# Decoder layer in fp32: softmax shift and sum moved into eight exponentials a unit

## The chip, the cores and the metric

One core of one Trainium2 chip runs the whole program. The metric is the device time in microseconds (us); lower is better. The engines are called PE (TensorE, matrix products), DVE (VectorE), ACT (ScalarE), POOL (GpSimd) and SP (SyncE, which issues the DMAs). They run their own instruction streams and meet through semaphores.

## The reference, cut to what matters

A post-norm decoder layer on x of shape (4, 256, 512): a masked dense product with gelu, a cross attention with 32 query and 8 key heads over 64 context positions, and a linear layer with routed low-rank additions, each followed by a residual sum and a normalization. All in fp32. The attention is the part that the change touches:

```
q = apply_rope((query @ wq) by head); k = apply_rope(key @ wk), v = value @ wv, each repeated 4 times
scores = einsum('bhqd,bhkd->bhqk', q, k) / sqrt(128)
attn   = softmax(scores + mask[:, None, :, :], axis=-1)      # over 64 keys
out    = einsum('bhqk,bhkd->bhqd', attn, v) ... @ wo
x = layernorm(x + out)
```

The softmax subtracts the row's maximum, takes the exponential and divides by the row's sum.

## The kernel before, in words

The program is one function, `decoder_layer`, with a block of instructions for each engine. The order on every engine is written out by hand, and each step waits for semaphores that count finished steps. Every fp32 product is three products of a high and a low part (`mm3`, lines 259 to 263), so most operands are split: ACT copies the high part (the `_hi` steps), DVE or POOL subtracts it to get the low part (the `_lo` steps).

The attention runs over eight head groups g = 0 to 7 (LAST is 7), one key head and four query heads each. Group 0 is written out ahead of the loop, groups 1 to 6 are turns of a loop (`Fori(1, LAST)`), and group LAST is written out behind it. A turn works on group g and finishes group g - 1. A group has four units u = 0 to 3 (two heads by one half of the 1024 tokens). For each unit:

- `query(g, u, f)`, f = 0 and 1: 12 matmuls of 512 columns on PE. `q_copy` (ACT), `q_sin` (POOL), `q_cos` and `q_rot` (DVE) apply the rotary embedding. f = 1 always uses PSUM bank 2, so the next one waits for `q_rot` of the last.
- `scores` (one unit) or `score_pair` (two): 64 matmuls of 64x64 a unit into banks 4 and 5.
- `mask_scores` (L1275, DVE, in place in PSUM), `row_max` (L1280), `shift` (L1287, subtracts the maximum, PSUM to the SBUF tile SM), `exps` (L897, ACT, one exponential of 512 columns), `row_sum` (L1292), `row_inverse` (L1296), then `probs` (L1728, POOL, multiplies by the inverse). The 512 columns of a unit are eight rows of 64 keys: four token tiles by two heads.
- `probs_transpose` (PE, four transposes), `pt_hi` (ACT) and `pt_lo` (DVE).

`value_out(g, n, b)`, n = 0 to 7, is 3 matmuls into bank b, which `vw_hi` (two ACT copies) and `vw_lo` (two DVE subtractions) split. `attend(g, t)`, t = 0 to 7, is 6 matmuls into a bank of A_BANKS, which `accumulate(g, t)` (DVE, L1314) adds to X. `keys` and `values` are 12 matmuls of 256 columns; `k_swap`, `k_sin`, `k_cos`, `k_add` and `k_spread` (four ACT copies) and `v_hi`, `v_lo` work on what they leave.

Behind the last group stand: `stats` and `guess` (DVE), `newton` and `mean_shift` (POOL) and `normalize` (ACT) for the second normalization; `weight_transpose` with `f_hi`, `f_lo`; `x2_tile(t)` (PE, four transposes) with `x2_hi` and `x2_lo`; `base(t)` (12 matmuls), `lora_in`, `lora_out(t)` (3 matmuls); then `out_add`, `stats(2, t)`, `guess(2, m)` on DVE, `newton(2, m)` on POOL for m = 0 to 2 and on DVE for m = 3 (in `out_last`), and the stores. `newton(2, 3)` waits for `newton(2, 2)`.

Of the kernel before, what the change touches and what calls it, by code (L numbers as in the profile page):

```python
# [12 lines left out]
ALU = mybir.AluOpType  # L13
# [18 lines left out]
def decoder_layer(nc, x, ctx_in, amask, w1, w2, b2, smask, wq, wk, wv, wo, fW, fb, fA, fB, rW, rb, rope, out):  # L32
# [24 lines left out]
    with ExitStack() as es:  # L57
# [51 lines left out]
        T_BANKS, A_BANKS = (7, 6, 7, 6), (6, 3, 6, 6, 6, 6, 3, 6)  # L109
# [5 lines left out]
        q_mm q_cp q_cos q_sin q_rot s_mm s_masked s_max s_sub s_exp s_sum s_inv p_done  # L115
# [43 lines left out]
        def x2_bank(t):  # L159
            return (5, 4, 3, 4, 3, 5, 3, 5)[t]  # L160
# [11 lines left out]
        def y_bank(t):  # L172
            return 2 + t % 2

# [83 lines left out]
        def _(pe):  # L258
# [214 lines left out]
            w2_transpose(3)  # L473
# [46 lines left out]
            pe.wait_ge(sm["tr_lo"], 8)  # L520
            values(0)
# [5 lines left out]
            dense(7)  # L527
            pe.wait_ge(sm["k_cos"], 1)
            query(0, 0, 0)
            pe.wait_ge(sm["tr_lo"], 14)  # L530
            value_out(0, 0, 7)
            pe.wait_ge(sm["x_added"], 7)
            query(0, 0, 1)
            pe.wait_ge(sm["tr_lo"], 13)
            x1_tile(4, 14)
            pe.wait_ge(sm["x_added"], 8)
            value_out(0, 1, 3)
            pe.wait_ge(sm["vw_lo"], n_vw(0, 0))
# [8 lines left out]
            pe.wait_ge(sm["tr_lo"], 15)  # L547
            x1_tile(6, 16)
            pe.wait_ge(sm["tr_lo"], 16)
            x1_tile(7, 17)  # L550
            pe.wait_ge(sm["q_rot"], n_rot(0, 0, 1))
            query(0, 1, 1)
            pe.wait_ge(sm["k_cos"], 1 + 1)
            query(0, 2, 0)
            pe.wait_ge(sm["tr_lo"], 18)
            value_out(0, 2, 7)
            pe.wait_ge(sm["vw_lo"], n_vw(0, 1))
            value_out(0, 3, 3)
            pe.wait_ge(sm["q_rot"], n_rot(0, 1, 1))
            query(0, 2, 1)  # L560
            pe.wait_ge(sm["vw_lo"], n_vw(0, 2))
# [3 lines left out]
            pe.wait_ge(sm["vw_lo"], n_vw(0, 3))  # L565
# [3 lines left out]
            pe.wait_ge(sm["s_sub"], n_unit(0, 0))  # L569
            scores(0, 1)  # L570
            pe.wait_ge(sm["pt_lo"], n_unit(0, 0))
            value_out(0, 5, 7)

            with pe.Fori(1, LAST) as g:
                pe.wait_ge(sm["k_cos"], g + 1)
                query(g, 0, 0)
                pe.wait_ge(sm["s_sub"], n_unit(g - 1, 1))
                score_pair(g - 1, 3)
                pe.wait_ge(sm["q_rot"], n_rot(g - 1, 3, 0))
                values(g)  # L580
                pe.wait_ge(sm["x_added"], n_added(g - 2, 7))
                probs_transpose(g - 1, 1)
                pe.wait_ge(sm["vw_lo"], n_vw(g - 1, 4))
                value_out(g - 1, 6, 3)
                pe.wait_ge(sm["q_rot"], n_rot(g - 1, 3, 1))
                query(g, 0, 1)
                pe.wait_ge(sm["pt_lo"], n_unit(g - 1, 1))
                attend(g - 1, 0)
                pe.wait_ge(sm["vw_lo"], n_vw(g - 1, 5))
                value_out(g - 1, 7, 7)  # L590
# [1312 lines left out]
```

## Time and profile before

| what | value |
|---|---|
| median of 3 runs | 492.2 us (491.89 to 492.32) |
| profiled execution, its own time | 492.99 us |
| its span (first to last instruction) | 491.2 us |
| mean granted clock of TensorE | 0.985 |
| busy: PE, DVE, ACT, POOL | 473.9, 408.3, 260.6, 273.4 us |
| read from HBM, written | 29.15 MB, 2.10 MB |

The profile is one execution. A row of a group names a line of the kernel, the engine, the operation and its tiles with their shapes, then how often it ran, its busy time, the mean time of one and the idle time of the engine just before it with what ended that. In a timeline each row has its start in the span, its duration, and in brackets the idle time before it and the step that ended it. The duration of a matmul is modelled and longer than the distance from one start to the next. The granted clock is a share of 2.4 GHz.

### The profile page before, as it was taken

The page shows a single profiled execution, that of the slowest core. Times are in us where ns is not written, and L with a number is a line of the kernel's source. Part 1 is how long each engine was busy: PE and PEld are TensorE (multiplying, and loading weights), DVE is VectorE, ACT ScalarE, POOL GpSimd, SP SyncE. Part 2 cuts the span into 40 slices and gives each one's busy share as a digit, 9 for nine tenths or more (in the row PEclk, how much of TensorE's full clock was granted, in tenths as well). Part 3 has the DMA queues.
Part 4 walks back from the last instruction along what each step waited for, and adds up shares of the span by engine and source line. Part 5 has one row for each costly group of instructions (what it writes and reads, how often), then busy time and mean ns, then how long its engine had stood idle before and what let it go on. Part 6 is the DMA issues. An engine that isn't in the chain of part 4 may idle for free.

```text
span 491.2 us, 11126 instructions
## 1 busy us (share of the span) xinstructions
PE 473.9 (96%) x4189; PEld 395.9 (81%) x4189; DVE 408.3 (83%) x739; ACT 260.6 (53%) x462; POOL 273.4 (56%) x347
## 2 busy tenths in 40 slices
PE   8999999999999999999999999999999999879991
PEld 8888778888888888888888888888888788668781
DVE  2779898988987898798979987988799889988585
ACT  4574447735673566365735663575458254353423
POOL 3477637854674467456636672676366423156523
PEclk9999999999999999999999999999999999979996
DMA  8943300240023011402040212022002400000013
GB/s 274 353 146 93 124 1 1 87 130 1 2 85 128 0 22 63 128 0 80 7 127 0 85 34 94 0 85 85 0 0 87 67 1 2 1 0 2 0 40 133
DMA packets 29137, 31.56 MB, mean 64 GB/s; under 512 B 6321, under 2 KB 16817, under 8 KB 29114
## 3 DMA queue, kind: packets, MB, share of 16 engines
q1 hardware_dynamic: 29114, 31.25, 20.1%
q8 instruction: 15, 0.25, 0.2%
q14 instruction: 8, 0.07, 0.0%
HBM read 29.15 MB, written 2.10 MB: 64 GB/s over the span
## 4 chain that ended last, share of the span: by engine, by line
PE 77%; DVE 9%; SPq 4%; POOL 3%; issue 3%; DMA 2%; ACT 1%; ACTq 0%; POOLq 0%; DVEq 0%
PE bank L261 23%; PE bank L263 22%; PE bank L262 22%; PE bank L369 6%; PE bank L393 3%; SPq L205 2%; DMA WQr<-in_L_xattn_wq_dram 2%; DVE X L1223 1%; DVE BST L1187 1%; PE bank L267 1%; POOL NW L1711 1%; DVE VWl L1139 1%; POOL NW L1709 1%; POOL RS L1713 1%; POOL NW L1707 1%
## 5 line engine op out<-in xcount | busy, mean ns | idle before, releaser
L1722 POOL TENSOR_TENSOR QS<-QS,SIN 128x512 f32<-128x512 f32 x64 | 83.0, 1297 | 124.4 <-ACT QS L801 124.4
L261 PE MATMUL bank<-XTh,WQh 128*128 128x512 f32 x256 | 101.7, 397 | 0.7 <-DVE XTl L1139 0.7
L263 PE MATMUL bank<-XTh,WQl 128*128 128x512 f32 x256 | 100.0, 391 | 0.0
L262 PE MATMUL bank<-XTl,WQh 128*128 128x512 f32 x256 | 99.7, 390 | 0.0
L1139 DVE TENSOR_TENSOR VWl<-bank,VWh 64x512 fp32r<-64x512 f32 x128 | 88.0, 688 | 9.3 <-ACT VWh L801 7.4
L801 ACT ACTIVATE QS<-bank 128x512 f32<-128x512 f32 x64 | 38.3, 598 | 103.1 <-PE bank L263 102.6
L801 ACT ACTIVATE VWh<-bank 64x512 fp32r<-64x512 f32 x128 | 75.9, 593 | 23.5 <-PE bank L263 20.9
L1251 DVE TENSOR_TENSOR bank<-bank,COS 128x512 f32<-128x512 f32 x64 | 44.6, 697 | 23.2 <-ACT QS L801 22.6
L261 PEld LDWEIGHTS bank<-XTh,WQh 128*128 128x128 f32 x256 | 48.1, 188 | 11.5 <-issue 1.3
L263 PEld LDWEIGHTS bank<-XTh,WQl 128*128 128x128 f32 x256 | 48.0, 188 | 10.5
L262 PEld LDWEIGHTS bank<-XTl,WQh 128*128 128x128 f32 x256 | 48.1, 188 | 9.5
L261 PE MATMUL bank<-VWh,PTh 128*128 128x512 f32 x128 | 50.9, 398 | 0.4 <-DVE X L1314 0.3
L262 PE MATMUL bank<-VWl,PTh 128*128 128x512 f32 x128 | 50.3, 393 | 0.0
L263 PE MATMUL bank<-VWh,PTl 128*128 128x512 f32 x128 | 50.1, 392 | 0.0
L1314 DVE TENSOR_TENSOR X<-X,bank 128x512 f32<-128x512 f32 x64 | 43.2, 674 | 7.2 <-PE bank L263 6.3
L1698 POOL TENSOR_TENSOR WOl<-WOr,WOh 128x512 fp32r<-128x512 f32 x32 | 41.3, 1291 | 12.1 <-ACT WOh L801 11.6
L1263 DVE TENSOR_TENSOR QR<-bank,QS 128x512 f32<-128x512 f32 x64 | 42.9, 683 | 0.4
L1688 POOL TENSOR_TENSOR WQl<-WQr,WQh 128x512 fp32r<-128x512 f32 x32 | 41.0, 1304 | 2.1 <-ACT WQh L801 2.1
L369 PEld LDWEIGHTS bank<-KK,QR 64*64 64x64 f32 x2048 | 31.6, 135 | 5.9 <-issue 5.8
L1728 POOL TENSOR_TENSOR SM<-SM,RI 128x512 f32<-128x512 f32 x32 | 33.5, 1046 | 3.8 <-DVE RI L1296 3.8
L369 PE MATMUL bank<-KK,QR 64*64 64x64 f32 x2048 | 34.2, 220 | 0.0
L261 PEld LDWEIGHTS bank<-VWh,PTh 128*128 128x128 f32 x128 | 24.3, 190 | 6.0 <-DVE X L1314 1.0
(150 smaller groups left out, 965.1 us busy)
## 6 DMA issues: line engine op xcount, KB each, us to landing
WQr<-in_L_xattn_wq_dram SPq DMA_DIRECT2D x8, 1024.0 KB, 5.5
WOr<-in_L_xattn_wo_dram SPq DMA_DIRECT2D x8, 1024.0 KB, 5.4
KVr<-in_L_xattn_wk_dram SPq DMA_DIRECT2D x8, 256.0 KB, 5.4
KVr<-in_L_xattn_wv_dram SPq DMA_DIRECT2D x8, 256.0 KB, 5.5
out_dram<-X SPq DMA_DIRECT2D x8, 256.0 KB, 2.0
X<-in_x_dram SPq DMA_DIRECT2D x3, 512.0 KB, 9.9
WQr<-in_L_attn_w_dram SPq DMA_DIRECT2D x4, 256.0 KB, 4.9
WOr<-in_L_attn_w_dram SPq DMA_DIRECT2D x4, 256.0 KB, 5.1
```

Source lines behind the costliest of these rows:

```text
L261: pe.matmul(o, lh, rh, start=start, stop=False)
L262: pe.matmul(o, lh, rl, start=False, stop=False)
L263: return pe.matmul(o, ll, rh, start=False, stop=stop)
L369: m = pe.matmul(s_tiles(u)[part, a, t, :], QR[head, u % 2, f, t * P + part.start:t * P + part.stop], KK[head, b, f, :], start=f == 0, stop ...
L801: return act.activation(o, i, ACT.Copy)
L1139: return dve.tensor_tensor(o, i, f32(hi), ALU.subtract)
L1251: dve.tensor_tensor(q, q, by_pos(COS, 2, S), ALU.mult).then_inc(sm["q_cos"], 1)
L1263: dve.tensor_tensor(QR[:, u % 2, f, :], bank[:, q_bank(u, f), :], QS[:, u % 2, 1 - f, :], ALU.add if f else ALU.subtract).then_inc(sm["q_r ...
L1314: dve.tensor_tensor(X[:, t, :], X[:, t, :], bank[:, A_BANKS[t], :], ALU.add)\
L1688: pool.tensor_tensor(wq_split(WQl, h), wq_head(WQr, h), f32(wq_split(WQh, h)), ALU.subtract)\
L1698: pool.tensor_tensor(WOl[:, h, :], WOr[:, h, :], f32(WOh[:, h, :]), ALU.subtract)\
L1722: pool.tensor_tensor(q, q, SIN[:, :].unsqueeze(1).broadcast_to([P, 2, S]), ALU.mult)\
```

## The change

The unit's softmax on DVE and ACT is arranged anew. `mask_scores` writes the masked scores to SBUF (the tile CTX, free after the context has been transposed) instead of back to PSUM. `row_max` reads them there and gives the negated maximum. `shift` and `row_sum` are gone. `exps` is eight exponentials of 64 columns, each with its row's negated maximum as bias and its sum as a second output; `row_inverse` waits for them. PE waits for `s_masked` where it waited for `s_sub`. Beside this the hand-written order of all engines is a new one, and PSUM banks are dealt out anew: all transposes of probabilities go to bank 7, and attends, value products and the transposes at the end use other banks. The matmuls are the same in number and shape.

The functions, then places of the new order that the prediction speaks of:

```diff
-        T_BANKS, A_BANKS = (7, 6, 7, 6), (6, 3, 6, 6, 6, 6, 3, 6)
+        T_BANKS, A_BANKS = (7, 7, 7, 7), (6, 6, 3, 7, 7, 7, 6, 3)
...
+        def masked_rows(u):
+
+            return CTX[:, u % 2, :].rearrange("p (a t k) -> p a t k", a=2, k=KS)
...
             def exps(g, u):
-                act.wait_ge(sm["s_sub"], UNITS * g + u + 1)
-                act.activation(SM[:, u % 2, :], SM[:, u % 2, :], ACT.Exp).then_inc(sm["s_exp"], 1)
+
+                act.wait_ge(sm["s_max"], n_unit(g, u))
+                if counted(UNITS * g + u - 1):
+                    act.wait_ge(sm["t_mm"], UNITS * g + u - 1)
+                for r in range(8):
+                    t, a = r // 2, r % 2
+                    m = act.activation(SM[:, u % 2, r * KS:(r + 1) * KS], masked_rows(u)[:, a, t, :], ACT.Exp,
+                                       bias=MX[:, u % 2, 4 * a + t:4 * a + t + 1], accum_out=SU[:, u % 2, r:r + 1])
+                m.then_inc(sm["s_exp"], 1)
...
-                s = s_tiles(u)
+                if counted(UNITS * g + u - 1):
+                    dve.wait_ge(sm["s_exp"], UNITS * g + u - 1)
...
-                dve.scalar_tensor_tensor(out=s, in0=s, scalar=1.0 / math.sqrt(DK), in1=m, op0=ALU.mult, op1=ALU.add)\
+                dve.scalar_tensor_tensor(out=masked_rows(u), in0=s_tiles(u), scalar=1.0 / math.sqrt(DK), in1=m, op0=ALU.mult, op1=ALU.add)\
...
-                dve.tensor_reduce(MX[:, u % 2, :].rearrange("p (a t) -> p a t", a=2), s_tiles(u), AX_X, ALU.max).then_inc(sm["s_max"], 1)
-
-            def shift(g, u):
...
+                dve.tensor_reduce(MX[:, u % 2, :].rearrange("p (a t) -> p a t", a=2), masked_rows(u), AX_X, ALU.max, negate=True).then_inc(sm["s_max"], 1)
+
+            def row_inverse(g, u):
                 dve.wait_ge(sm["s_exp"], UNITS * g + u + 1)
-                dve.tensor_reduce(SU[:, u % 2, :], sm_rows(u), AX_X, ALU.add).then_inc(sm["s_sum"], 1)
```

The turn of the loop in the changed kernel, by engine, without the waits (g1 is g - 1):

```
PE:  query(g,0,0) attend(g1,1) score_pair(g1,3) value_out(g1,7) query(g,0,1) values(g) attend(g1,2) attend(g1,3)
     query(g,1,0) probs_transpose(g1,2) value_out(g,0) query(g,1,1) probs_transpose(g1,3) query(g,2,0) value_out(g,1)
     attend(g1,4) score_pair(g,1) value_out(g,2) attend(g1,5) query(g,2,1) attend(g1,6) attend(g1,7)
     probs_transpose(g,0) value_out(g,3) query(g,3,0) value_out(g,4) query(g,3,1) probs_transpose(g,1) keys(g+1)
     value_out(g,5) value_out(g,6) attend(g,0)
ACT: q_copy(g,0,0) k_spread(g) vw_hi(g1,7) exps(g1,2) v_hi(g) q_copy(g,0,1) exps(g1,3) wo_hi(g,3) wkv_hi(g+1)
     q_copy(g,1,0) pt_hi(g1,2) vw_hi(g,0) q_copy(g,1,1) pt_hi(g1,3) q_copy(g,2,0) vw_hi(g,1) vw_hi(g,2) exps(g,0) ...
DVE: q_cos(g,0,0) accumulate(g1,1) mask_scores(g1,2) row_max(g1,2) mask_scores(g1,3) row_max(g1,3) vw_lo(g1,7)
     row_inverse(g1,2) v_lo(g) q_cos(g,0,1) accumulate(g1,2) accumulate(g1,3) q_rot(g,0,0) row_inverse(g1,3) q_rot(g,0,1) ...
```

The hand-over behind the last scores, before and after:

```
PE before:  scores(L,3) attend(L,3) value_out(L,5) value_out(L,6) weight_transpose(2) value_out(L,7) weight_transpose(3)
            probs_transpose(L,3) x2_tile(0) x2_tile(1) weight_transpose(4) attend(L,4) base(0) attend(L,5) ...
PE after:   scores(L,3) weight_transpose(1) probs_transpose(L,2) attend(L,0) weight_transpose(2) value_out(L,4) attend(L,1)
            weight_transpose(3) attend(L,2) value_out(L,5) weight_transpose(4) attend(L,3) value_out(L,6)
            probs_transpose(L,3) value_out(L,7) x2_tile(0) attend(L,4) attend(L,5) attend(L,6) attend(L,7) x2_tile(1) base(0) ...
DVE after:  mask_scores(L,3) row_max(L,3) f_lo(1) pt_lo(L,2) accumulate(L,0) stats(1,0) row_inverse(L,3) f_lo(2)
            accumulate(L,1) vw_lo(L,4) stats(1,1) accumulate(L,2) guess(1,0) f_lo(3) vw_lo(L,5) accumulate(L,3) stats(1,2)
            vw_lo(L,6) pt_lo(L,3) stats(1,3) vw_lo(L,7) guess(1,1) x2_lo(0) accumulate(L,4) ...
ACT after:  ... pt_hi(L,2) exps(L,3) f_hi(2) vw_hi(L,4) f_hi(3) vw_hi(L,5) f_hi(4) vw_hi(L,6) pt_hi(L,3) vw_hi(L,7) normalize(1,0) ...
```

At the end, and in the head:

```diff
             lora_out(2)
             lora_out(3)
+            pe.wait_ge(sm["fy_out"], 2)
+            base(6)
             lora_out(4)
             lora_out(5)
-            pe.wait_ge(sm["fy_out"], 2)
-            base(6)
-            lora_out(6)
             pe.wait_ge(sm["fy_out"], 4)
             base(7)
+            lora_out(6)
             lora_out(7)
...
             out_add(3)
+            stats(2, 3)
+            guess(2, 1)
             out_add(4)
-            stats(2, 3)
+            stats(2, 4)
             out_add(5)
-            stats(2, 4)
-            guess(2, 1)
             stats(2, 5)
+            guess(2, 2)
             out_add(6)
-            guess(2, 2)
...
             dense(6)
-            pe.wait_ge(sm["tr_lo"], 8)
-            values(0)
+            pe.wait_ge(sm["tr_lo"], 7)
+            keys(0)
```

## Rows read from the trace of the kernel before

**Rows 1.** Page: busy time by engine; slices of PE and of its clock.
```profile
PE 473.9 (96%) x4189; PEld 395.9 (81%) x4189; DVE 408.3 (83%) x739; ACT 260.6 (53%) x462; POOL 273.4 (56%) x347
...
PE   8999999999999999999999999999999999879991
...
PEclk9999999999999999999999999999999999979996
```

**Rows 2.** Busy time of PE, PEld, DVE, ACT, POOL in two stretches, then granted clock.
```profile
183.77:231.05 47.28, 47.28 (x468) 39.70 (x471) 40.49 (x67) 26.61 (x49) 28.44 (x24) 1.00 0.18 55
433.00:439.00 6.00, 5.37 (x21) 5.01 (x22) 4.75 (x10) 3.55 (x6) 3.00 (x3) 0.50 0.00 0
```

**Rows 3.** Timeline of PE around the last scores and after: start, duration.
```profile
423.32 1.16 PE L369 MATMUL bank<-KK,QR 64*64 64x64 f32 x64
...
429.93 0.50 PE L261 MATMUL bank<-WOh,VTh 128*128 128x512 f32 x1 [1.69 <-DVE VWl L1139]
...
433.63 1.08 PE L393 MATMUL bank<-ID,SM 128*128 128x128 f32 x4 [2.30 <-POOL SM L1728]
...
442.19 0.39 PE L261 MATMUL bank<-VWh,PTh 128*128 128x512 f32 x1
442.42 0.39 PE L262 MATMUL bank<-VWl,PTh 128*128 128x512 f32 x1
```

**Rows 4.** Chain that ended last: start, time in it, of 64 small matmuls and 4 transposes.
```profile
84.52 1.09 PE bank L369 x64
...
92.88 0.44 PE bank L393 x4
```

**Rows 5.** Timeline of DVE in the same stretch: start, duration, idle before.
```profile
424.63 0.69 DVE L1275 SCALAR_TENSOR_TENSOR bank<-bank,MSK 128x512 f32<-128x512 f32 x1
425.23 0.68 DVE L1187 BATCH_NORM_STATS2 BST<-X 128x6 f32<-128x512 f32 x1
...
426.05 0.66 DVE L1280 TENSOR_REDUCE MX<-bank 128x8 f32<-128x512 f32 x1
...
427.82 0.16 DVE L1196 TENSOR_SCALAR VE<-MV 128x2 f32<-128x2 f32 x1
...
428.48 1.39 DVE L1139 TENSOR_TENSOR VWl<-bank,VWh 64x512 fp32r<-64x512 f32 x2
429.91 0.69 DVE L1292 TENSOR_REDUCE SU<-SM 128x8 f32<-128x512 f32 x1
...
439.65 0.69 DVE L1314 TENSOR_TENSOR X<-X,bank 128x512 f32<-128x512 f32 x1 [1.75 <-PE bank L263]
```

**Rows 6.** Groups of DVE by line: busy us, mean ns of one, idle before.
```profile
L1275 DVE SCALAR_TENSOR_TENSOR bank<-bank,MSK 128x512 f32<-128x512 f32 x32 | 22.2, 692 | 2.0 <-PE bank L369 1.8
L1287 DVE TENSOR_TENSOR SM<-bank,MX 128x512 f32<-128x512 f32 x32 | 21.9, 684 | 0.3
...
L1292 DVE TENSOR_REDUCE SU<-SM 128x8 f32<-128x512 f32 x32 | 21.6, 676 | 0.8 <-ACT SM L897 0.7
```

**Rows 7.** Groups of ACT: exponential, short copies, one with two pointers, shortest one.
```profile
L897 ACT ACTIVATE SM<-SM 128x512 f32<-128x512 f32 x32 | 20.0, 626 | 5.3 <-DVE SM L1287 5.3
...
L801 ACT ACTIVATE KK<-KC 64x256 f32<-64x256 f32 x32 | 13.3, 416 | 9.0 <-PE bank L369 7.7 <-POOL KC L1742 1.0
...
L926 ACT ACTIVATE X<-X,NM,RS 128x512 f32<-128x512 f32 x8 | 6.2, 808 | 10.2 <-POOL NM L1760 10.2
...
L931 ACT ACTIVATE LG<-LG 4x8 f32<-4x8 f32 x1 | 0.2, 208 | 3.2 <-DVE LG L1353 3.2
```

**Rows 8.** Timeline of ACT, two operations one behind the other.
```profile
414.71 0.58 ACT L801 ACTIVATE QS<-bank 128x512 f32<-128x512 f32 x1
415.19 0.60 ACT L801 ACTIVATE PTh<-bank 128x512 fp32r<-128x512 f32 x1
```

**Rows 9.** Timeline of DVE at the end.
```profile
481.08 0.69 DVE L1378 TENSOR_TENSOR X<-X,bank 128x512 f32<-128x512 f32 x1 [0.47 <-PE bank L263]
...
485.25 0.46 DVE L1215 TENSOR_SCALAR NW<-RS,VH 128x1 f32<-128x1 f32 x2 [1.85 <-POOL RS L1713]
```

More of the change, by code:

```diff
@@ L568, in _ @@
             query(0, 3, 1)
-            pe.wait_ge(sm["s_sub"], n_unit(0, 0))
-            scores(0, 1)
             pe.wait_ge(sm["pt_lo"], n_unit(0, 0))
-            value_out(0, 5, 7)
+            probs_transpose(0, 1)
+            pe.wait_ge(sm["q_rot"], n_rot(0, 2, 0))
+            keys(1)
+            pe.wait_ge(sm["vw_lo"], n_vw(0, 4))
+            value_out(0, 5, 3)
+            pe.wait_ge(sm["pt_lo"], n_unit(0, 1))
+            value_out(0, 6, 7)
+            pe.wait_ge(sm["vw_lo"], n_vw(0, 3))
+            attend(0, 0)
             with pe.Fori(1, LAST) as g:
@@ L689, in _ @@
+            query(LAST, 3, 1)
+            pe.wait_ge(sm["s_masked"], n_unit(LAST, 1))
+            scores(LAST, 2)
+            pe.wait_ge(sm["vw_lo"], n_vw(LAST, 3))
+            weight_transpose(0)
+            pe.wait_ge(sm["pt_lo"], n_unit(LAST, 0))
             attend(LAST - 1, 5)
             pe.wait_ge(sm["vw_lo"], n_vw(LAST, 2))
-            value_out(LAST, 3, 7)
-            pe.wait_ge(sm["vw_lo"], n_vw(LAST, 1))
             attend(LAST - 1, 6)
             pe.wait_ge(sm["x_added"], n_added(LAST - 1, 5))
-            attend(LAST - 1, 7)
@@ L1417, in _ @@
             residual(2)
+            x_lo(6, 7)
             stats(0, 2)
@@ L1515, in _ @@
                 q_cos(g, 2, 0)
-                accumulate(g - 1, 3)
-                vw_lo(g, 0, 7)
+                vw_lo(g, 1, 3)
+                accumulate(g - 1, 4)
                 mask_scores(g, 0)
-                pt_lo(g - 1, 3)
                 row_max(g, 0)
-                vw_lo(g, 1, 3)
-                shift(g, 0)
+                mask_scores(g, 1)
+                vw_lo(g, 2, 3)
+                accumulate(g - 1, 5)
+                row_max(g, 1)
+                row_inverse(g, 0)
@@ L1603, in _ @@
-            row_sum(LAST, 2)
-            q_cos(LAST, 3, 0)
+            f_lo(0)
+            accumulate(LAST - 1, 5)
+            q_rot(LAST, 3, 0)
+            accumulate(LAST - 1, 6)
+            q_rot(LAST, 3, 1)
             row_inverse(LAST, 2)
             pt_lo(LAST, 1)
-            vw_lo(LAST, 4, 3)
-            q_cos(LAST, 3, 1)
+            accumulate(LAST - 1, 7)
+            mask_scores(LAST, 3)
+            row_max(LAST, 3)
+            f_lo(1)
             pt_lo(LAST, 2)
             accumulate(LAST, 0)
-            q_rot(LAST, 3, 0)
@@ L1612, in _ @@
             stats(1, 0)
-            q_rot(LAST, 3, 1)
+            row_inverse(LAST, 3)
+            f_lo(2)
             accumulate(LAST, 1)
-            f_lo(1)
+            vw_lo(LAST, 4, 7)
+            stats(1, 1)
             accumulate(LAST, 2)
-            mask_scores(LAST, 3)
-            stats(1, 1)
-            row_max(LAST, 3)
+            guess(1, 0)
+            f_lo(3)
+            vw_lo(LAST, 5, 6)
             accumulate(LAST, 3)
-            shift(LAST, 3)
-            guess(1, 0)
@@ L1623, in _ @@
-            vw_lo(LAST, 5, 7)
-            row_sum(LAST, 3)
-            f_lo(2)
-            row_inverse(LAST, 3)
+            stats(1, 2)
             vw_lo(LAST, 6, 3)
-            stats(1, 2)
-            vw_lo(LAST, 7, 7)
-            f_lo(3)
             pt_lo(LAST, 3)
+            stats(1, 3)
+            vw_lo(LAST, 7, 6)
+            guess(1, 1)
             x2_lo(0)
-            stats(1, 3)
             accumulate(LAST, 4)
-            guess(1, 1)
             f_lo(4)
-            x2_lo(1)
```

729 lines of the change are left out of this document (343 added, 386 removed).

## The prediction

> **What bounds the kernel now.** I read the page first. TensorE (PE) is busy 473.9 of 491.2 us and its slices are full nearly throughout [rows 1]. A busy PE alone says little, so I read its timeline: in a dense stretch a 128x512 matmul starts every 0.23 us (442.19, 442.42) though its row says 0.39 [rows 3]. Counting in such pitches (0.227 for 512 columns, 0.44 for four transposes, 1.09 for the 64 small matmuls of one unit of scores [rows 4]) the loop leaves PE next to nothing: a turn takes 47.28 us with PE busy all of it, DVE 40.49 and ACT 26.61 [rows 2]. One turn is 8 queries (2.73 each), 8 attends (1.36), 8 value products (0.68), two projections (1.4), four units of scores and four sets of transposes, some 46.8. So VectorE (DVE) relief in the loop is worth at most 0.5 us a turn, and probably nothing.
>
> PE loses time at three places only. First, the head, some 2 us over the first 70. Second, the hand-over from the last head group to the feed-forward part: between the end of scores(LAST,3) (423.32 + 1.09 = 424.41) and the start of attend(LAST,5) (442.19) lie 17.8 us [rows 3]. PE's work in it is attend 2 x 1.36, value_out 3 x 0.68, weight_transpose 3 x 0.44, probs_transpose 0.44, x2_tile 2 x 0.44, base 2.73: 10.1. So 7.7 us are lost: 1.69 idle for a VectorE subtraction, 2.30 for POOL's probabilities [rows 3], and 433 to 439 runs at a granted clock of 0.50, the 1.2 GHz level, with 5.37 us busy [rows 2], half of it (2.7) lost. DVE works without a break there, until 1.75 us idle before 439.65 [rows 5]. Third, the end: after the last matmul the closing Newton steps on DVE start at 485.25, after 1.85 us of waiting for POOL [rows 9].
>
> **The change, DVE's side.** Every unit loses shift and row_sum, 684 and 676 ns [rows 6]; behind other work an operation costs 0.60 (424.63 to 425.23 [rows 5]). That is 1.2 us a unit, 4.8 a turn, 38 in all. mask_scores now writes SBUF and row_max reads it; row_sum already read SBUF at 676 beside 684 for a PSUM operand [rows 6], so I take no change, 0.05 us either way.
>
> **ACT's side.** One exponential of 512 columns (626 ns) becomes eight of 64. 128x512 costs 626 and 64x256 costs 416 [rows 7]: 0.82 ns a column and 206 ns fixed, so 259 for 64 columns. Two pointer operands (bias and scale) make 808 of 626 [rows 7], so the bias alone adds 91: 350 ns. Operations one behind the other overlap by 0.11 (414.71 to 415.19 with 0.58 [rows 8]): 0.24 each, 2.0 us a unit. The running sum is nowhere in this trace. Below, it costs nothing (e, the time of a unit's exponentials, is 2.0). Above, it is a whole instruction like the shortest here, 208 ns [rows 7], with every overlap lost: 558 ns, e = 4.5. I take a short instruction that overlaps like the others, 0.10, so 0.34 each and e = 2.8, since all neighbours in this trace overlap. A gain from the sum itself is excluded: it adds work to ACT.
>
> The Trainium skill (ScalarE: Activation LUTs, Rules for kernel authors) speaks against splitting: it budgets 0.3 us for each ACTIVATE with a bias pointer plus 0.83 ns an element, which would make 2.8 us a unit before any sum. By the rows it is 2.0 before the sum, because of the overlap. The skill gives no price for the sum on this engine.
>
> **In the loop.** ACT goes from 26.6 to 26.6 - 2.5 + 11.2 = 35.3 of 47.3 us, DVE to 35.7. Neither reaches PE. What counts is that an ACT block of length e delays the copies queued behind it. The tightest place I find: after score_pair(g-1,3) PE has value_out, query, values, two attends, query, a transpose and a value_out, 11.4 us, before query(g,1,1), which waits for q_rot(g,0,1) to free its bank. Against that stand k_spread 1.7 (four of 416 [rows 7]), vw_hi 1.1, exps e, v_hi 0.4, q_copy 0.5, exps e again, and on DVE row_inverse and q_rot, 0.85, since row_inverse(g-1,3) is queued ahead of that q_rot. 4.55 + 2e is at most 11.4 while e is at most 3.4. At 2.8 the loop stays PE's; every 0.1 beyond 3.4 costs 0.2 a turn. The next tightest, probs_transpose(g,0), is 7.5 us behind its scores and needs 4.2 + e. T_BANKS all 7 adds waits for pt_lo before the transposes of the next unit; they have over 0.5 us to spare in that walk.
>
> **At the hand-over.** PE's order is new: scores(LAST,3) comes earlier, and twelve blocks (9.7 us) instead of six stand between it and its transpose, so the wait for POOL (2.30) is covered. But what is late next is DVE. From mask_scores(LAST,3) to accumulate(LAST,4), which attend(LAST,5) now needs at once as both use bank 7, DVE's order holds: mask 0.72, ten single operations 6.0, four stats 3.3 (0.82 from 425.23 to 426.05), two guesses 1.3 (0.66 from 427.82 to 428.48), four vw_lo pairs 5.7 (1.43 from 428.48 to 429.91) [rows 5], row_inverse 0.11, x2_lo(0) 0.76, accumulate 0.69: 18.6 us. PE's work from the end of the scores to that attend is 12.6: 6.0 us late. DVE starts 0.4 late, and f_lo(2), queued behind exps(LAST,3) on ACT, is in time only for e up to 2.1: 0.7 more at 2.8. In all 7.1 lost, spread over several gaps of 1 to 2 us where before it was 2 large ones.
>
> The clock cost 2.7 us here before. After gaps of this size together I expect the 1.2 GHz level again, partly while PE would wait for DVE anyway: 2.0, between 0 and 3. The Trainium skill (TensorE: Matmul & The Clock Gate, What's actually happening) says that the gate follows how busy PE has been recently; the trace agrees, the low level begins after the idle 2.30 us. So hand-over: 7.1 + 2.0 - 7.7 = +1.4.
>
> **At the ends.** After: lora_out(6) and (7) come last on PE, and guess(2,1), guess(2,2) earlier on DVE. DVE then does out_add, stats, out_add, stats, guess after the last but one product: 480.4 + 0.72 + 0.83 + 0.72 + 0.90 + 0.64 = 484.2, and POOL, fed by guess(2,2) at some 479.9, is done at 483.8 (3.9 us of Newton and mean). The closing steps start at 484.2 instead of 485.25 [rows 9]: -1.0. In the head keys(0) moves behind dense(6); the first transposes of normalized tiles then wait some 1.8 us for Newton steps where 2 were lost: 0, give or take 1. Mask and DMA issues don't move.
>
> Sum: 0 (loop) + 1.4 - 1.0 + 0 = +0.4. The profiled execution took 493.0 with a span of 491.2; the median of the runs is 492.2, and I add the difference to that: 492.6.
>
> **Rivals.** (A) ACT becomes what PE waits for in the loop. If reading the sum can't overlap (e from 3.4 to 4.5), q_rot(g,0,1) comes late: at e = 3.9 that is 2 x 0.5 x 6 turns = 6, plus 1.1 at the hand-over: 500; at 4.5 some 507. It decides from e = 3.4, 0.42 us an exponential. For it: nothing in the trace shows such a sum hidden. Against: every neighbour overlaps.
> (B) The clock holds. With e near 2.1 and shorter gaps the hand-over loses 6.4 and no clock: 6.4 - 7.7 - 1.0 = -2.3, about 489.9. For it: the 2.30 gap is gone. Against: DVE's 18.6 us against 12.6.
>
> **How the numbers follow.** A measurement of this kernel can tell about 0.2% (1 us) from no change. The forecast, 492.6 with its own range 491 to 495, has 0.45: of that 0.06 faster, 0.22 within, 0.17 slower. A has 0.27, all slower; B 0.28, all faster. Faster 0.34, same 0.22, slower 0.44. The range takes in B down to 489 and A up to e = 3.9, 500; beyond lie 0.07 and 0.12.
>
> **What would show it.** The loop turn: 47.3 us means e under 3.4; over 48 means A, and then PE's waits name QR or ACT's copies. A unit's exponentials, first start to last end: 2.0, 2.8 or over 3.4. Rows of a separate instruction for the sum, with their duration. Between scores(LAST,3) and the fourth attend of the second half PE's waits should name DVE (f_lo, accumulate, vw_lo), not POOL, and the granted clock there tells forecast from B. At the end the closing Newton steps should start about 3.5 us behind the last matmul, not 4.6. I am wrong if the hand-over loses much less than 7 us, which would mean that DVE enters it with fewer operations left than I count, or if the loop turn changes with e under 3.4.

## The result, and the profile after

| | before | after |
|---|---|---|
| median, us (lowest to highest) | 492.32 (491.89 to 493.34, 7 runs) | 496.21 (494.55 to 498.38, 7 runs) |
| ratio to before, 95% interval | | 1.0077 [1.0054, 1.0101] |
| profiled execution, us | 492.99 (span 491.2) | 498.38 (span 496.6) |

The change makes the kernel 3.9 us slower. The range of the prediction holds it (489.0 to 500.0), its likeliest value, 492.6, lies 3.6 us too low. The profiled execution of after is the slowest of its seven, so a second profile of the same kernel stands beside it (below, r1): 495.06 us, span 493.3. Where the two disagree, I say so.

The page of after, busy time, the slices of PE and of its clock, and two groups, which answer to [rows 1, 6, 7]:

```profile
PE 477.0 (96%) x4189; PEld 396.2 (80%) x4189; DVE 371.1 (75%) x675; ACT 325.6 (66%) x942; POOL 273.6 (55%) x347
...
PE   8999998899999999999999999999999999879992
...
PEclk9999999999999999999999999999999999969998
...
L906 ACT ACTIVATE SM<-CTX,MX 128x64 f32<-128x64 f32 x256 | 85.3, 337 | 3.1 <-DVE MX L1292 2.9
...
L906 ACT ACTIVATION_READ_ACCUMULATOR SM<-CTX,MX 128x1 f32 x256 | 48.6, 190 | 0.0
```

DVE lost 37.2 us of work and ACT gained 65.0, and neither shows in the end time: the loss of 3.9 us lies elsewhere. The last group is the answer to a question that the trace of before left open: the sum is an instruction of its own, 190 ns, behind each exponential. What the two cost together is read from the timeline of ACT (start, duration), where one unit begins:

```profile
417.50 0.35 ACT L906 ACTIVATE SM<-CTX,MX 128x64 f32<-128x64 f32 x1 [0.40 <-DVE MX L1292]
417.76 0.19 ACT L906 ACTIVATION_READ_ACCUMULATOR SM<-CTX,MX 128x1 f32 x1
417.85 0.33 ACT L906 ACTIVATE SM<-CTX,MX 128x64 f32<-128x64 f32 x1
418.09 0.19 ACT L906 ACTIVATION_READ_ACCUMULATOR SM<-CTX,MX 128x1 f32 x1
418.18 0.34 ACT L906 ACTIVATE SM<-CTX,MX 128x64 f32<-128x64 f32 x1
```

From 417.50 over 417.85 to 418.18: a pair every 0.33 us, the two overlapping their neighbours by 0.1. The next operation on ACT, a copy, starts 8 pairs later, at 420.17, so e, the time of a unit's exponentials, is 2.67 us. One turn of the loop (busy time of PE, PEld, DVE, ACT, POOL, then granted clock), beside [rows 2]:

```profile
117.76:165.16 47.40, 47.40 (x466) 39.73 (x465) 35.70 (x59) 34.72 (x108) 28.36 (x25) 1.00 0.18 56
```

The turn is 47.40 us for 47.28, with PE busy all of it, DVE at 35.70 and ACT at 34.72. Then the waits of PE over the whole span (us in total, times, longest):

```profile
PE bank L271 <- ACT X L937: 2.2, 1, 2.2
...
PE bank L397 <- DVE X L1314: 1.5, 1, 1.5
PE bank L265 <- DVE QR L1274: 1.5, 1, 1.5
PE bank L265 <- issue: 1.3, 1, 1.3
PE bank L265 <- DVE VWl L1150: 1.1, 2, 0.6
PE bank L265 <- DVE X L1314: 0.8, 1, 0.8
```

Every one happens once or twice; none belongs to the loop. Four waits are the hand-over (2.2, 1.5, one of the two for VWl, 0.8), seen in PE's timeline, which answers to [rows 3]:

```profile
432.61 0.39 PE L267 MATMUL bank<-WOh,VTl 128*128 128x512 f32 x1
434.49 0.66 PE L397 MATMUL bank<-ID,SM 128*128 128x128 f32 x4 [1.50 <-DVE X L1314]
...
438.06 1.09 PE L271 MATMUL bank<-ID,X 128*128 128x128 f32 x4 [2.21 <-ACT X L937]
439.63 0.76 PE L265 MATMUL bank<-VWh,PTh 128*128 128x512 f32 x1 [0.49 <-DVE VWl L1150]
440.20 0.63 PE L266 MATMUL bank<-VWl,PTh 128*128 128x512 f32 x1
...
443.31 0.79 PE L265 MATMUL bank<-VWh,PTh 128*128 128x512 f32 x1 [0.78 <-DVE X L1314]
```

POOL's probabilities are gone as a releaser. In their place stand accumulate(LAST,3), normalize(1,0) on ACT, vw_lo(LAST,7) and accumulate(LAST,4). From 440.20 a 512-column matmul takes 0.43 us from start to start instead of 0.23: the 1.2 GHz level. The granted clock falls at 437.4, inside the wait of 2.2 us (in before at 432.4, inside the wait of 2.30), and not behind it. How long the low level lasts differs between executions (windows; the columns as above):

```profile
439.00:448.00 9.00, 7.73 (x19) 5.54 (x19) 6.45 (x14) 2.12 (x3) 4.10 (x15) 0.52 0.00 1
```

in the profiled execution of after, all of 437.4 to 447.6, but in r1 only 437.8 to 441.2:

```profile
438.00:441.00 3.00, 2.71 (x6) 1.82 (x6) 2.00 (x7) 0.00 (x0) 1.96 (x7) 0.50 0.00 0
```

At the end the last matmul starts at 487.05 and the closing Newton steps of DVE, as in [rows 9], start 3.6 us later; in before these were 480.65 and 485.25, 4.6 us:

```profile
487.05 0.39 PE L267 MATMUL bank<-WOh,PTl 128*128 128x512 f32 x1
```
```profile
490.68 0.46 DVE L1226 TENSOR_SCALAR NW<-RS,VH 128x1 f32<-128x1 f32 x2
```

**Where the time went.** I take PE's timeline and subtract from the distance between two entries the pitches of its matmuls (0.227 us for 512 columns, 0.1185 for 256, 0.11 for a transpose, 0.0158 for a 64x64). What is left is time lost on PE, in us:

| stretch | before | after, profiled | r1 | why |
|---|---|---|---|---|
| 0 to 70 | 4.9 | 4.7 | 4.9 | head |
| 70 to 120 (group 0, first turn) | 0.9 | 4.3 | 2.8 | q_rot(0,2,1) 1.65; in one of them an "issue" gap 1.4 |
| 120 to 420 (loop) | 4.2 | 4.3 | 4.4 | nothing over 0.3 at a place |
| 420 to 460 (hand-over) | 8.4 | 11.0 | 9.4 | four waits, and 0.7 at a weight_transpose; 1.2 GHz |
| 460 to the last matmul | 0.8 | 1.2 | 0.8 | |
| last matmul to the end of the span | 10.3 | 9.3 | 9.3 | closing Newton earlier |

Taken from the spans, 491.2, 496.6 and 493.3, the sums of the columns leave 461.7, 461.8 and 461.7 us of work for PE: the same work to within 0.1 us, so the table accounts for the loss. A turn loses 0.50 us by these pitches in before and 0.62 in after; the six turns' 0.7 us is mostly made up by the straight code behind the loop.

### The profile page after: what moved, and what is told of

It is laid out like the page before. It is cut to its first block, busy times and chain, and to the rows that moved or that the text cites. A ratio compares the mean times of both kernels' runs of the same rounds, so it can differ in the third digit from the quotient of the medians.

```text
span 496.6 us, 11523 instructions
## 1 busy us (share of the span) xinstructions
PE 477.0 (96%) x4189; PEld 396.2 (80%) x4189; DVE 371.1 (75%) x675; ACT 325.6 (66%) x942; POOL 273.6 (55%) x347
## 4 chain that ended last, share of the span: by engine, by line
PE 90%; DVE 6%; ACT 2%; issue 1%; POOL 0%; POOLq 0%; DVEq 0%; ACTq 0%
PE bank L265 26%; PE bank L267 25%; PE bank L266 25%; PE bank L373 6%; PE bank L397 3%; DVE VWl L1150 2%; PE bank L271 2%; PE bank L286 1%; ACT SM L906 1%; DVE BST L1198 1%; DVE X L1314 1%; PE bank L279 0%; DVE QR L1184 0%; ACT VWh L805 0%; PE bank L326 0%
## 5 line engine op out<-in xcount | busy, mean ns | idle before, releaser
L906 ACT ACTIVATE SM<-CTX,MX 128x64 f32<-128x64 f32 x256 | 85.3, 337 | 3.1 <-DVE MX L1292 2.9
L265 PE MATMUL bank<-VWh,PTh 128*128 128x512 f32 x128 | 52.0, 406 | 1.3 <-DVE X L1314 0.8
L267 PE MATMUL bank<-VWh,PTl 128*128 128x512 f32 x128 | 51.1, 399 | 0.0
L906 ACT ACTIVATION_READ_ACCUMULATOR SM<-CTX,MX 128x1 f32 x256 | 48.6, 190 | 0.0
```

The costliest lines, as they stand in the source:

```text
L265: pe.matmul(o, lh, rh, start=start, stop=False)
L267: return pe.matmul(o, ll, rh, start=False, stop=stop)
L906: m = act.activation(SM[:, u % 2, r * KS:(r + 1) * KS], masked_rows(u)[:, a, t, :], ACT.Exp, bias=MX[:, u % 2, 4 * a + t:4 * a + t + 1], a ...
```

## The experiments

Each ratio is to the kernel before on the same chip, with its 95% interval.

**The same kernel again** (label r1_after_again).

> The changed kernel once more, on the chip of the next three. Its profiled execution was its slowest run (498.4 beside a median of 496.2), so one trace may hold what is not in all of them. Theory 1 (the hand-over is paced by DVE's order and the clock falls there): about 10 to 11 us lost between 420 and 450 again, and the one idle stretch of 1.28 us that the trace puts down to nothing at 97.5 may be missing. Theory 2 (the loss is spread and random): the hand-over's loss differs by over 2 us from 10.9. Time 1.006 to 1.010 of the kernel before.

496.1 us, 1.0079 [1.0062, 1.0096]: the loss is the kernel's, not that of one session. The profile of this run has the 1.65 us in front of query(0,3,1), the four waits of the hand-over and the turn of 47.40 us as after has, but no gap with "issue" and only 3.4 us at 1.2 GHz.

**Softmax and order apart.** The change does two things at once, so each was made alone. e1 has the new softmax in the old order of work on all engines (shift and row_sum struck out, the rest where it stood):

```diff
 def row_inverse(g, u):
-    dve.wait_ge(sm["s_sum"], UNITS * g + u + 1)
+    dve.wait_ge(sm["s_exp"], UNITS * g + u + 1)
...
-                shift(g, 0)
...
-                row_sum(g, 0)
```

> The new softmax (shift and row_sum gone, eight exponentials) in the old order and the old banks. Theory 1 (the new order of the hand-over is what costs): the loop turn stays at 47.3 as a unit's exponentials take 2.7 us, DVE has 1.2 us a unit less in the hand-over, so the loss there is under the 7.7 of before, some 5 to 7, and the time is 0.995 to 1.001 of before. Rival (the eight exponentials cost, whatever the order): 1.005 or more, with waits of PE for QR or VW tiles whose ACT copies stand behind exponentials.

506.44 us, 1.0282 [1.0265, 1.0299]: the rival is right, though the tile that is late in the loop is VTl and not one of those it named. A turn takes 48.79 us, and PE is idle in it for the first time:

```profile
188.86:237.65 48.79, 47.59 (x466) 39.61 (x465) 35.73 (x59) 34.65 (x109) 28.34 (x25) 1.00 0.16 54
```
```profile
PE bank L265 <- DVE VTl L1150: 7.4, 6, 1.4
PE bank L397 <- POOL SM L1704: 3.6, 2, 2.6
```

DVE and ACT are as little busy as in after (35.7 and 34.7); only the places differ. In the old order v_hi stands behind exps on ACT, and the long block (its timeline of this turn runs exponentials from 195.28 to 197.94, then WOh, QS, and VTh only at 199.08) makes v_lo late by up to 1.4 us in each of six turns. e2 is the other half, the old softmax in the new order (shift put back behind each row_max on DVE, row_sum ahead of each row_inverse):

> The old softmax (shift behind row_max, row_sum ahead of row_inverse, one exponential of 512) in the new order and banks. Theory 1 (the new order's hand-over is paced by DVE): slower than the changed kernel, as DVE gets 2 x 0.6 us more between mask_scores(LAST,3) and accumulate(LAST,4) though the exponential is 2 us shorter: loss in the hand-over 11 to 13, time 1.008 to 1.015 of before. Rival (the exponentials are what costs): at or under 1.002 of before.

503.53 us, 1.0232 [1.0214, 1.0249], more than either expectation, as both took the loop to be free; a turn takes 48.21 us, with the loss at another place:

```profile
165.93:214.14 48.21, 47.57 (x466) 39.57 (x465) 40.70 (x67) 26.62 (x48) 28.28 (x25) 1.00 0.17 54
```
```profile
PE bank L393 <- DVE X L1314: 5.6, 8, 1.5
```

The accumulate that the transposes wait for stands behind operations that the new order doesn't allow for. So +2.8% and +2.3% apart are +0.8% together: the new order is what lets the loop carry a block of 2.67 us on ACT, and with the old softmax, placed as it is here, it loses. Other places for shift and row_sum weren't tried.

**Without the sum.** e5 leaves the row sums out (the divisor is a constant 1.0), so its output isn't the reference's; all else is that of after:

```diff
-    bias=MX[...], accum_out=SU[:, u % 2, r:r + 1])
+    bias=MX[...])
```

> The changed kernel without the sums of the exponentials: each of the eight has its bias but no second output, the tile of sums is set to 1.0 once, so the probabilities are not divided by their sum (that part of the computation is left out). The 256 accumulator reads are gone. A unit should take 8 x 0.24 = 1.9 instead of 2.67 us. Theory 1 (loop turn bound by PE, hand-over by DVE, f_lo(2) behind the exponentials): turn stays 47.4, hand-over loses some 0.7 less, 0.998 to 0.999 of the changed kernel. Rival (the eight exponentials are what costs): 0.995 or less of it.

496.49 us, 1.0081 [1.0064, 1.0098]: striking 256 instructions of 190 ns (48.6 us of busy ACT) gives nothing that can be measured, though the intervals would still hide the 0.5 to 1 us that was expected. The eight exponentials start 0.24 us apart now (the block runs from 70.13 to 72.06, e = 1.93), and at one place PE feels that: the wait ahead of query(0,3,1), 1.5 us in after, is half as long,

```profile
PE bank L265 <- DVE QR L1274: 0.7, 1, 0.7
```

which other gaps of that profile take up (one with "issue" is 2.0 us).

**How long a block ACT can have.** e4 computes twelve exponentials a unit (four again, into a spare buffer, with their sums), e11 ten:

```diff
+    for r in range(4):          # 2 in e11
+        m = act.activation(DUM[:, u % 2, r * KS:(r + 1) * KS], masked_rows(u)[...], ACT.Exp,
+                           bias=MX[...], accum_out=DSU[:, u % 2, r:r + 1])
```

> The changed kernel with twelve exponentials a unit instead of eight (four more with sums, into scratch that nobody reads): a unit takes 12 x 0.333 = 4.0 us. It tests the threshold of the prediction (3.4 us). By its walk query(g,1,1) comes 2 x 0.6 = 1.2 us late in each of six turns: turn 48.4 to 48.8 instead of 47.4, the wait put down to q_rot (QR), hand-over 1.3 us worse, in all 8 to 10 us, 1.016 to 1.020 of the changed kernel. Rival (the walk leaves out slack): turn unchanged at 47.4 and only the hand-over worse, 1.003 of it.

> Ten exponentials of 64 columns a unit instead of eight (two go to a spare buffer), so that a unit's block on ScalarE is 3.3 us. With twelve (4.0 us) a loop turn took 49.9 us, 2.5 more. Theory 'the threshold is at 3.4 as worked out, but all four blocks of a turn count': the turn stays at 47.4 to 47.6, ratio to before 1.008 to 1.013. Rival 'the threshold lies near 2.7, where the kernel stands, at 2 us a turn for each us': the turn takes 48.5 to 48.7, ratio 1.022 to 1.026.

| exponentials | e, us | turn, us | lost ahead of query(0,3,1), us | median, us | ratio |
|---|---|---|---|---|---|
| 8, no sums (e5) | 1.93 | 47.40 | 0.90 | 496.49 | 1.0081 |
| 8 (after) | 2.67 | 47.40 | 1.65 | 496.21 | 1.0077 |
| 10 (e11) | 3.33 | 47.79 | 2.30 | 503.57 | 1.0212 [1.016, 1.0265] |
| 12 (e4) | 4.00 | 49.89 | 2.97 | 519.43 | 1.0548 [1.0531, 1.0566] |

(e at 0.333 us a pair, the losses from PE's timeline, pitches subtracted.) The fourth column grows by 1.0 us for each us of e: in group 0 one block of exponentials lies on the path of PE in every one of these kernels, and there is no threshold down to 1.93. The load of ACT's table stands directly ahead of that block, exps(0,0). In after row_max(0,0) is done at 69.62, and the load is what ACT does until 71.25:

```profile
69.97 1.28 ACT L906 ACT_TABLE_LOAD   x1
```

In before it lies under the work of DVE, as the exponential waits longer for shift:

```profile
71.60 1.28 ACT L897 ACT_TABLE_LOAD   x1
73.24 0.63 ACT L897 ACTIVATE SM<-SM 128x512 f32<-128x512 f32 x1 [0.36 <-DVE SM L1287]
```

So some 1.3 of the 1.65 us may be the load's; this is an estimate from these rows, and no run moved it. Windows of a turn, ten and twelve:

```profile
168.59:216.38 47.79, 47.49 (x464) 39.70 (x465) 35.54 (x59) 37.10 (x124) 28.19 (x24) 1.00 0.17 55
```
```profile
195.87:245.76 49.89, 48.50 (x465) 39.46 (x465) 35.55 (x59) 39.73 (x140) 28.11 (x25) 1.00 0.16 53
```

The walk of the prediction put the threshold at e = 3.4 and the slope behind it at 0.2 us a turn for each 0.1 of e. The threshold is a little high: at 3.33 a turn is already 0.39 longer, and the place is one that the walk didn't name, score_pair(g,1), late in every turn of e11:

```profile
168.59 2.10 PE L374 MATMUL bank<-KK,QR 64*64 64x64 f32 x128 [0.29 <-DVE QR L1279]
```

So it lies between 2.67 and 3.33. The slope is steeper: between 3.33 and 4.00 a turn grows by 2.10, 3.1 us for each us of e, not 2. In e4 the bank that the walk named, that of query(g,1,1), is late in every turn (210.66):

```profile
210.66 0.50 PE L266 MATMUL bank<-XTh,WQh 128*128 128x512 f32 x1 [0.58 <-DVE QR L1279]
...
219.22 2.10 PE L374 MATMUL bank<-KK,QR 64*64 64x64 f32 x128 [0.32 <-DVE QR L1279]
...
239.41 0.50 PE L266 MATMUL bank<-WOh,VTh 128*128 128x512 f32 x1 [0.33 <-DVE PTl L1155]
```

but it isn't alone: query(g,1,0) behind v_lo, score_pair(g,1) and value_out(g,6) behind pt_lo wait as well. Four blocks that count in full beyond 3.4 would give 4 x (4.0 - 3.4) = 2.4 for the 2.49 measured, but nothing at 3.33; which blocks add up isn't shown. e4 is 4.7% over after, where its expectations had 1.6 to 2.0% or 0.3%.

My expectation for e11 had 47.4 to 47.6 for the turn and 1.008 to 1.013 for the ratio, and neither holds: only 2.3 of its 7.4 us over after lie in the loop. By the profiled executions (spans 504.2 and 496.6) 4.0 more are lost between 70 and 120 and 1.4 more around the hand-over. Of the 4.0, 0.65 lie ahead of query(0,3,1) and 0.55 in a gap with "issue". The rest is TensorE's clock, which is at 1.2 GHz twice there, first 1.2 us behind the wait ahead of query(0,3,1) and again behind the "issue" gap:

```profile
83.40:86.80 3.40, 3.40 (x11) 2.53 (x10) 2.00 (x4) 2.66 (x9) 2.21 (x2) 0.50 0.00 0
100.50:103.90 3.40, 3.40 (x9) 2.62 (x9) 1.39 (x3) 3.36 (x20) 0.00 (x0) 0.50 0.01 2
```

PE has dense work in both, so each costs some 1.5 us. In e4 the clock is low from 83.2 to 86.6, too; in after and r1 it stays at 1.00 in group 0. In e11 and e4 the longer wait is thus followed by a stretch at 1.2 GHz, which comes on top of the wait.

**The new end alone.** e3 is the kernel before with nothing of the change but the order of the last four lora_out and of out_add, stats and guess on DVE:

```diff
                 out_add(3)
+                stats(2, 3)
+                guess(2, 1)
                 out_add(4)
-                stats(2, 3)
+                stats(2, 4)
                 out_add(5)
-                stats(2, 4)
-                guess(2, 1)
                 stats(2, 5)
+                guess(2, 2)
                 out_add(6)
-                guess(2, 2)
```

> The kernel before with the new order of the end alone: base(6) ahead of lora_out(4) and (5), lora_out(6) and (7) last, and the new order of out_add, stats and guess on DVE. Theory 1 (as worked out in the prediction): the closing Newton steps start 3.5 us behind the last matmul, not 4.6, and the time falls by 1.0 us, ratio 0.998. Rival (the POOL steps end no earlier): no change, ratio 1.000.

491.32 us over 10 runs, 0.9978 [0.9968, 0.9987]: 1.0 us faster than before, as expected. This part of the change is a gain, and after has it too.

**The clock at the hand-over.** Fillers are 128x128 matmuls of the identity into bank 5, which nothing uses there; they keep PE busy while it would wait. e6 puts 34 of them into after (10, 16, 3 and 5 ahead of the four waits):

```diff
+            fill(10)
             pe.wait_ge(sm["x_added"], n_added(LAST, 3))
             probs_transpose(LAST, 3)
...
+            fill(16)
             pe.wait_ge(sm["vw_lo"], n_vw(LAST, 6))
             x2_tile(0)
```

> The changed kernel with 34 idle-time matmuls of 128 columns (identity by identity into PSUM bank 5, read by nobody) in front of the four waits of the hand-over, so that PE is busy there. They add work and change nothing else. Theory 1 (about a third of the hand-over's loss is the low clock and not the waits): the granted clock stays at 1.00, the waits for DVE stay, and 2 to 3.5 us come back: 0.993 to 0.996 of the changed kernel, 492.5 to 494 us. Rival (DVE's order alone paces the hand-over): the clock is held and the time stays within 0.8 us.

494.28 us, 1.0050 [1.0029, 1.0071], 1.8 us under the repeat of after, where 2 to 3.5 was expected. The granted clock stays at 1.00:

```profile
436.00:442.00 6.00, 6.00 (x44) 5.57 (x44) 4.39 (x12) 1.24 (x2) 3.23 (x11) 1.00 0.01 3
```

The waits themselves are still there, under the fillers. The gain of 1.8 us is one of medians from two sessions, whose intervals overlap (1.0029 to 1.0071 and 1.0062 to 1.0096). The traces say where a clock can cost anything here. In r1 and in e6 attend(LAST,5) starts at

```profile
441.97 0.51 PE L265 MATMUL bank<-VWh,PTh 128*128 128x512 f32 x1 [0.78 <-DVE X L1314]
```
```profile
440.80 0.47 PE L265 MATMUL bank<-VWh,PTh 128*128 128x512 f32 x1
```

which is 22.32 and 22.30 us behind the start of scores(LAST,3) (419.65 and 418.50); in after, too, it is 22.32. Up to there the waits for the other engines set the pace, whatever the clock. Behind it stand dense attends. From scores(LAST,3) to the last matmul it takes 64.04 us in e6, 64.09 in r1, whose clock is back before attend(LAST,5), and 66.06 in the profiled execution of after, whose clock is low until 447.6. So the low clock costs 2.0 us in that execution and nothing in the one of r1. What it costs before is the next question. e8 does the same in e3, with 30 fillers (12 ahead of value_out(LAST,7), 18 ahead of probs_transpose(LAST,3)):

> The kernel before with the new order of the end (that alone gave 0.9978) and with 30 such matmuls ahead of value_out(LAST,7) and probs_transpose(LAST,3), where PE is idle for 1.7 and 2.3 us. Theory 1: the clock stays high between 432 and 439, 2 to 2.7 us come back, in all 0.993 to 0.994 of before, 488.6 to 489.2 us. Rival (the waits behind, on DVE, only take up what the clock gives): 0.997 to 0.998, the end's share alone.

491.94 us over 10 runs, 0.9986 [0.9976, 0.9996], no gain over e3. The trace shows that this was no test of the clock. A filler takes 0.22 us, so 30 take 6.6, and PE had only 4.0 us to wait there [rows 3]. The transposes of the probabilities started at 436.37, which is 12.56 us behind the start of scores(LAST,3), for 10.31 in before (433.63 and 423.32):

```profile
436.37 0.60 PE L398 MATMUL bank<-ID,SM 128*128 128x128 f32 x4
```

e9 has 7 and 10 in their place:

```diff
+            fill(7)
             pe.wait_ge(sm["vw_lo"], n_vw(LAST, 5))
             value_out(LAST, 7, 7)
...
+            fill(10)
             pe.wait_ge(sm["x_added"], n_added(LAST, 3))
             probs_transpose(LAST, 3)
```

> The kernel before with the new order of the end and 17 filler matmuls instead of 30 (7 before value_out(LAST,7), 10 before probs_transpose(LAST,3), some 0.22 us each), so that they end when the weights and the probabilities come. Theory 'the low clock costs': the granted clock stays at 1.00 over 430 to 440, attend(LAST,4) comes 2 us earlier, and the time falls from 491.3 by 1.5 to 2.5, ratio to before 0.993 to 0.995. Rival 'VectorE has the last word there': attend(LAST,5) starts where it did, 441.6, and the ratio is that of the new end alone, 0.997 to 0.999.

490.22 us, 0.9961 [0.9944, 0.9979], 1.1 us under e3 and 6 under after: the lowest median of this study. The interval overlaps that of e3, and the gain lies between the two expectations. The clock is at 1.00 throughout,

```profile
433.00:439.00 6.00, 5.16 (x31) 4.28 (x30) 5.62 (x15) 2.82 (x6) 2.67 (x4) 1.00 0.01 3
```

the transposes start at 433.22, as in e3 (433.23), and attend(LAST,5) at 440.15 instead of e3's 441.61, with scores(LAST,3) at 422.93 in both. That is 1.5 us earlier, less than the 2.7 that the low clock took from PE there: a wait of 0.79 us for pt_lo(LAST,3) on DVE takes up part, as its row shows:

```profile
PE bank L261 <- DVE PTl L1147: 0.8, 1, 0.8
```

So the clock costs 1.8 us in after and 1.1 in e3, which has before's hand-over, by the medians, and 0 to 2.0 and 1.5 by the traces; the difference of the two isn't clear of noise. But e6 and e9, both at full clock, are still 4.1 apart (494.28 and 490.22, intervals apart), of the 4.9 between after and e3 (496.2 and 491.3). Most of the loss is not the clock's.

**Two repairs of after.** e10 moves one line: base(0), 2.73 us of matmuls, from behind x2_tile(1) to between attend(LAST,4) and attend(LAST,5), where before has it.

```diff
             attend(LAST, 4)
+            pe.wait_ge(sm["f_lo"], 2)
+            base(0)
             pe.wait_ge(sm["x_added"], n_added(LAST, 4))
```

> The changed kernel with one line moved: base(0), 2.73 us of matmuls, stands between attend(LAST,4) and attend(LAST,5), as it does in the kernel before, instead of behind x2_tile(1). Theory 'part of the hand-over's loss is work put behind a wait that it could have covered': the wait of attend(LAST,5) for accumulate(LAST,4), 1.2 us, is gone, the clock rises again no later, and the time falls from 496.2 by 1 to 1.5, ratio to before 1.005 to 1.006. Rival 'VectorE's queue sets the end of this stretch anyway': the wait comes back at attend(LAST,6), (7) or base(1), ratio unchanged at 1.008.

497.19 us, 1.0099 [1.0079, 1.0119]: the rival is right, and the change from 1.0079 isn't clear of noise. The wait for accumulate(LAST,4) has gone from the list and another of 1.5 us has come, x2_tile(2) for x2_lo on DVE:

```profile
PE bank L271 <- DVE XTl L1150: 1.5, 1, 1.5
```

e12 takes the wait in group 0. In after, q_rot(0,2,1), which query(0,3,1) waits for, stands behind mask_scores(0,1), row_max(0,1) and pt_lo(0,0) on DVE; e12 puts both q_rot ahead of them:

```diff
+            q_rot(0, 2, 0)
+            q_rot(0, 2, 1)
             mask_scores(0, 1)
             row_max(0, 1)
-            q_rot(0, 2, 0)
             pt_lo(0, 0)
-            q_rot(0, 2, 1)
```

> The changed kernel with group 0's q_rot(0,2,0) and q_rot(0,2,1) ahead of mask_scores(0,1) and row_max(0,1) in VectorE's queue. Theory 'the 1.65 us that TensorE loses ahead of query(0,3,1) is VectorE's order': q_rot(0,2,1) ends 1.9 us earlier, the gap is gone, and the time falls from 496.2 by 1.2 to 1.6, ratio to before 1.0045 to 1.006. Rival 'the scores of unit 1 are late instead': the probabilities and transposes of unit 1 come 1.2 us later, PE waits there, ratio 1.008.

498.55 us, 1.0128 [1.0108, 1.0148], slower by 2.4, more than the rival had. The wait of 1.5 us for QR is gone, and PE waits for unit 1's probabilities:

```profile
PE bank L397 <- POOL SM L1704: 2.4, 1, 2.4
```

Mask and maximum come 0.9 us later than in after (80.34 for 79.47), and the chain of exponentials, row_inverse and POOL's product behind them has no slack. The wait that came is 0.9 us longer than the one that went (2.4 for 1.5); the rest of the 2.4 isn't shown, beyond an "issue" gap of 1.0 us in this profile. In group 0 the units' softmax and the rotations compete for one DVE, and one of them is late.

## Why the prediction was right or wrong

**Size of the block on ACT: right.** e was put at 2.8 (2.0 to 4.5) and is 2.67. The sum is a separate short instruction that overlaps its neighbours by 0.1, as taken; 0.34 us a pair was predicted, 0.33 is measured. The budget of the Trainium skill (ScalarE: Activation LUTs, Rules for kernel authors) gives an estimate of 2.8 us without any sum; the traces have 1.93 without it (e5) and 2.67 with it. That 2.8 stands in both places is chance.

**Loop: right.** PE busy for the whole turn, 47.40 us; ACT at 34.7 (35.3 predicted), DVE at 35.7 (35.7). The relief of DVE by 4.8 us a turn was worth nothing, as said. (The terms of the turn add up to 47.1 and not to 46.8, so at most 0.2 us a turn was to be had, not 0.5.) The turn is 0.12 us longer; what that is, no run shows. The margin was real too, but smaller: rival A begins between 2.67 and 3.33, shown by after and e11, at another place than the walk's tightest one. Its slope is steeper (e4), and it would have cost more than "500 at e = 3.9".

**Hand-over: the mechanism right, the size short.** The prediction had "7.1 lost, spread over several gaps of 1 to 2 us", plus 2.0 for the clock, 9.1 in all, against 7.7 before. Counted as it counts, from the end of scores(LAST,3) to attend(LAST,5), after, r1 and e6 have 21.2 us with 12.6 of work: 8.6 lost to waits, 1.5 more than the walk. The clock comes behind that stretch and adds 2.0 in the profiled execution of after, nothing in r1. So the hand-over is +0.9 to +2.9 for the +1.4 forecast (+1.0 to +2.6 by the table above). DVE is the releaser of three of the four waits, and POOL of none, as said. One releaser was missed, normalize(1,0) on ACT, the longest wait (2.2): in ACT's queue it stands behind two pairs of vw_hi copies, the second of which needs PE's value_out(LAST,7) (435.88 and 437.10 in its timeline), and the walk had followed DVE only. The clock term of 2.0 was met by one execution and not by the other. What I set against it was too large: the 2.7 us of before, half of the busy time at 1.2 GHz, are worth only 1.1 in the median and 1.5 at attend(LAST,5) when PE is kept busy (e9), as DVE was the next to be waited for.

**Group 0: the step that failed.** "In the head keys(0) moves behind dense(6) ... 0, give or take 1." I looked at the head up to the first transposes and at the loop, and walked nothing of the straight code of group 0 between them. There PE loses 1.65 us ahead of query(0,3,1) (82.73 in after, 1.49 of it a wait for QR), and in before nothing of the kind between 70 and 120. The chain can be read in after: the load of ACT's table from 69.97, exps(0,0) from 71.27 to 73.94, two pairs of vw_hi and two q_copy behind it until 77.6, and on DVE what follows them, with mask_scores(0,1), row_max(0,1) and pt_lo(0,0) ahead of q_rot(0,2,1) at 81.99. It is the walk that I did for the loop, with a slack below zero. This 1.65 is the part of the miss that both profiles of after's code have in the same size. That it lies on the path of PE is shown by the waits that follow e one for one; that 1.65 us of time would come back without it isn't, since e12 took it away and another wait came.

**End: right.** -1.0 us in after, r1 and e3.

**Sum.** In the order of the table, r1 has 0.0 (head), +1.9 (70 to 120, of that the 1.65), +0.2 (120 to 420), +1.0 (hand-over) and -1.0 (end): +2.1, where +0.4 was forecast. The profiled execution of after has -0.2, +3.4, +0.1, +2.6, +0.4 (460 to the last matmul) and -1.0: +5.3; it holds the "issue" gap of 1.4 (below) and the 2.0 of the clock on top. On the profiled execution of before, 492.99, these give 495.1 and 498.3; measured are 495.06 and 498.38. The forecast's own range, 491 to 495, doesn't hold the median of 496.21. The whole range does, because rival A stretched it to 500, and A's mechanism, ACT as what PE waits for in the loop, is absent at e = 2.67. To that extent the hit is luck.

## What to carry to other kernels

Work that is taken from an engine with slack gives nothing, however much it is; walk the straight code ahead of and behind a loop as closely as the loop, with every engine's queue, since there the same change costs where the loop has slack to hide it. An operation that gets longer needs its followers moved out from behind it, and then order and operation fit only each other: here each alone cost about three times what both together did. Where TensorE must wait anyway and its clock falls, the low clock costs only as far as dense work follows: look for that before filling the wait with matmuls of no use, and add not one more than fit (here 17 gave some 1.1 us, 30 gave nothing).

## What the runs showed of the hardware

The running sum of an exponential on ScalarE isn't free but cheap: a separate ACTIVATION_READ_ACCUMULATOR of 190 ns, which moves the start of the next exponential from 0.24 to 0.33 us; the 64-column exponential itself takes 337 ns with bias, where I had 350.

After the same waits of the hand-over, the 1.2 GHz level lasted 10.2 us in one execution (after), 3.4 in another of the same kernel (r1), and 6.8 in e12. What decides it, these runs don't show. In r1 and e12 it cost nothing that the traces show (64.09 and 64.03 us from scores(LAST,3) to the last matmul, for 64.04 in e6 at full clock), in after 2.0 us.

A gap of 1.0 to 2.0 us with "issue" as its releaser, thus with nothing that the profile shows, stands near 95 to 98 us in after, e2, e5, e11 and e12, ahead of a query product (e11's at 100.29):

```profile
98.77 0.50 PE L265 MATMUL bank<-XTh,WQh 128*128 128x512 f32 x1 [1.28 <-issue]
```

r1, e4, e6 and e10, which have the same order there as after, don't show it, nor does any profile of a kernel in the old order (before, e1, e3, e8, e9). Its cause stays open; no run was made for it.
